# One chunk in 28 of two edge sums read row by row by the queues of ScalarE and SyncE

## What is computed

```python
def _gnn_layer(x, row, col, W, b, g, beta):
    neigh = x[col]
    agg = jax.ops.segment_sum(neigh, row, num_segments=n)
    deg = jax.ops.segment_sum(jnp.ones((row.shape[0],), x.dtype), row, num_segments=n)
    deg = jnp.maximum(deg, 1.0)[:, None]
    h = (x + agg / deg) @ W.T + b
    ...
x = _gnn_layer(x, row, col, W0, b0, g0, beta0)
x = _gnn_layer(x, row, col, W1, b1, g1, beta1)
```

## Time and profile before

| | us |
|---|---|
| median of three runs | 7440.92 |
| lowest and highest | 7439.2, 7442.39 |
| the profiled execution | 7400.07 |
| its span, first to last instruction | 7398.1 |
| granted TensorE clock, mean share of full | 0.714 |
| busy: PE, VectorE, POOL, ScalarE | 3606.4, 2823.8, 3772.0, 831.4 |

### The profile page before, as it was taken

The page is one execution under the profiler, slowest core; times in us unless marked ns, Lnnn a source line. Parts: engine busy times, 40 slices in busy tenths (PEclk is TensorE's granted clock), DMA queues, the critical chain, the costliest instruction groups (busy, mean ns, idle before and its releaser), DMA issues. The chain is left out here.

```text
span 7398.1 us, 63577 instructions
## 1 busy us (share of the span) xinstructions
PE 3606.4 (49%) x13693; PEld 2603.5 (35%) x13694; DVE 2823.8 (38%) x6837; ACT 831.4 (11%) x2066; POOL 3772.0 (51%) x3797
## 2 busy tenths in 40 slices
PE   4113965444433445445331222299992455555529
PEld 1001543333322333333230000078881344344317
DVE  5116854444435344444380000011114455555761
ACT  0001930000002000000130000022221100000222
POOL 4772046666662666666507777700005566667221
PEclk7556987777766777777655555599996777778759
DMA  3001023333311333332012000022214333333140
GB/s 134 1 0 37 13 58 92 93 92 91 92 42 47 92 91 93 92 93 84 5 38 91 2 4 4 9 72 81 81 57 135 90 91 92 90 90 92 55 160 18
DMA packets 290129, 497.38 MB, mean 67 GB/s; under 512 B 99253, under 2 KB 182880, under 8 KB 290048
## 3 DMA queue, kind: packets, MB, share of 16 engines
q0 software_dynamic: 163264, 345.19, 16.5%
q1 hardware_dynamic: 125696, 150.28, 6.3%
q10 hardware_dynamic: 1088, 1.05, 0.1%
HBM read 487.50 MB, written 92.89 MB: 78 GB/s over the span
## 5 line engine op out<-in xcount | busy, mean ns | idle before, releaser
L956 PE MATMUL sum_sums<-sum_got,sum_onehot 128*128 x4992 | 1627.4, 487 | 1717.5 <-DVE acc L1118 1317.3
L888 POOL DMA_INDIRECT sum_got<-xn,edge_row x1568 | 1539.5, 982 | 1139.8 <-issue 450.4
L956 PEld LDWEIGHTS sum_sums<-sum_got,sum_onehot 128*128 128x128 f32 x4992 | 1173.7, 245 | 2153.5 <-issue 1944.0
L1118 DVE TENSOR_TENSOR acc<-acc,sum_sums 128x257 f32 (+1 forms) x2496 | 1053.2, 422 | 1775.8 <-remote 1242.6
L888 POOL DMA_INDIRECT sum_got<-h,edge_row x784 | 753.9, 962 | 484.0 <-issue 226.3
L1256 POOL DMA_INDIRECT table<-rec,addr x784 | 807.8, 1030 | 291.5 <-issue 275.4
L1763 PE MATMUL moe_f_ps_y<-xb,moe_f_hT 128*128 128x256 f32 x1792 | 475.9, 398 | 297.7 <-issue 297.6
L1747 PE MATMUL moe_f_ps_h<-moe_f_xT,xb 128*128 128x256 f32 x1792 | 473.7, 398 | 286.5 <-issue 286.3
L1828 DVE TENSOR_TENSOR moe_f_y<-moe_f_ps_y,moe_b 128x256 f32<-128x256 f32 x112 | 42.3, 420 | 1337.2 <-PE moe_f_ps_y L1763 650.1
L1595 POOL DMA_INDIRECT moe_out_c_got<-moe_out,place_i x98 | 95.7, 976 | 826.2 <-PEq L1553 787.9
L1256 POOL DMA_INDIRECT table<-sort_rec,sort_addr x392 | 400.4, 1022 | 202.1 <-issue 122.5
(11 more groups left out here) (481 smaller groups left out, 3432.2 us busy)
## 6 DMA issues: line engine op xcount, KB each, us to landing
xb<-in_L_ffn_W SPq DMA_DIRECT2D x112, 1024.0 KB
sum_got<-xn,edge_row POOLq DMA_INDIRECT x1568
moe_in<-acc SPq DMA_DIRECT2D x28, 512.0 KB
moe_f_xin<-moe_in SPq DMA_DIRECT2D x56, 256.0 KB
moe_out<-moe_f_y SPq DMA_DIRECT2D x56, 256.0 KB
xn<-xb SPq DMA_DIRECT2D x14, 896.0 KB
table<-rec,addr POOLq DMA_INDIRECT x784
sum_got<-h,edge_row POOLq DMA_INDIRECT x784
```

What stands on the lines that cost most here:

```text
L888: pool.indirect_dma_start(got[:, c % SU, 0:D], None, source, bass.IndirectOffsetOnAxis(ap=p.edge_row[:, c:c + 1], axis=0)).then_inc(s_got[ ...
L956: mm = nc.tensor.matmul(sums[k % 2][j], onehot[:, (k % QUARTERS) * HALF + j, :], flat(got[:, bass.ds(where[n % PLAN], 1), :]), start=True, ...
L1118: v.tensor_tensor(a, a, sums[k % 2][j], ALU.add).then_inc(s_added[j], 1)
```

## The change

In sum0 and sum1, POOL leaves out the last chunk of each turn. Its 128 rows are fetched by 128 DMAs of one row each, whose row numbers are read into registers from a list: rows 0 to 71 by ACT's queue, in three batches of 24, rows 72 to 127 by SP's, in four batches of 14. The chunk has a slot of its own in odd turns (`got` has 29 slots), and the plan names the other slot for them, for which VectorE has three more operations. The row numbers stand in device memory in `row_list`, which SP writes once in sum0 (3584 numbers of 4 bytes, out of `edge_row`) and both engines read from, 72 or 56 numbers for each turn. ACT begins a turn's rows when `s_free` reaches four times the turn's number less 4, and in sum0 after its last clear. SP issues 14 rows behind each group's `s_landed`: behind the first two the second half of the turn under way, behind the last two the first half of the next. Before its first gate it issues the first half of turn 0. A turn counts as landed when both the 27 gathers and the 128 rows are in. Sum2 is not touched. Over both sums ACT issues 4032 such DMAs, SP 3136, and the lists take 112 small ones; POOL issues 56 gathers less.

```diff
@@ -44,6 +44,9 @@
 QW = CH
 BLOCK = 112
 BLOCKS = CH // BLOCK
+TURNS = CH // SU
+BY_ACT, ACT_BATCH = 72, 24
+BY_SP, SP_BATCH = 56, 14
 SE = 7
 FLYING = 7
 
@@ -727,7 +730,7 @@
     return eng.snap(register, min_val=1, max_val=most)
 
 
-def sum_over_edges(p, source, order, weighted, table, own=None):
+def sum_over_edges(p, source, order, weighted, table, own=None, by_row=None):
 
 
 
@@ -735,7 +738,10 @@
     with ExitStack() as ctx:
         cols = D if weighted else D + 1
         fields = 2 if weighted else 1
-        got = p.sb("got", [P, SU, cols], F32, ctx)
+
+
+        last_slot = SU - 1
+        got = p.sb("got", [P, SU + (by_row is not None), cols], F32, ctx)
         onehot = p.sb("onehot", [P, QUARTERS * HALF, P], F32, ctx)
         spare = p.sb("spare", [P, 4], F32, ctx)
 
@@ -752,6 +758,11 @@
         s_added = [s(f"s_added{j}") for j in range(HALF)]
         s_ready, s_built, s_onehot, s_sum = s("s_ready"), s("s_built"), s("s_onehot"), s("s_sum")
         s_landed, s_free = s("s_landed"), s("s_free")
+        if by_row is not None:
+            act_numbers, sp_numbers = p.sb("act_numbers", [1, 2, BY_ACT], I32, ctx), p.sb("sp_numbers", [1, 2, BY_SP], I32, ctx)
+            s_listed, s_room, s_known = s("s_listed"), s("s_room"), s("s_known")
+            s_act_list, s_sp_list, s_rows = ([s(f"{name}{odd}") for odd in range(2)]
+                                             for name in ("s_act_list", "s_sp_list", "s_rows"))
         if own is not None:
             own_rhs, own_biases = own
             own_row, own_flip = p.sb("own_row", [P, 2, D], F32, ctx), p.sb("own_flip", [P, 2, D], F32, ctx)
@@ -817,22 +828,71 @@
         def _(sp):
             if table is not None:
                 sp.dma_start(raw, table.rearrange("(p q) a -> p q a", p=P)).then_inc(s_raw, 16)
+            if by_row is not None and table is not None:
+                sp.wait_ge(s_table, 1)
+                sp.dma_start(by_row.rearrange("(c p) -> p c", p=P),
+                             p.edge_row[:].rearrange("p (c u) -> p c u", u=SU)[:, :, SU - 1],
+                             allow_slow_non_contiguous=True).then_inc(s_listed, 16)
+                sp.wait_ge(s_listed, 16)
+            if table is not None:
                 sp.wait_ge(s_plan, 3)
 
-            def step(i):
+            def read_list(turn, odd):
+                sp.dma_start(sp_numbers[:, odd, :], by_row[bass.ds(2 * P * turn + odd * P + BY_ACT, BY_SP)].unsqueeze(0)
+                             ).then_inc(s_sp_list[odd], 16)
+
+            def read_rows(turn, odd, quarter):
+                if quarter == 0:
+                    gate(sp, s_sp_list[odd], 16 * turn + 16, s_known)
+                first = quarter * SP_BATCH
+                _, row = nc.values_load_multi_w_load_instructions(
+                    sp_numbers[:, odd, first:first + SP_BATCH], (mybir.EngineType.SP,),
+                    min_val=0, max_val=NT * P - 1, skip_runtime_bounds_check_because="they are rows of the source")
+                for u in range(SP_BATCH):
+                    at = BY_ACT + first + u
+                    sp.dma_start(got[at:at + 1, last_slot + odd, 0:D],
+                                 source[bass.ds(row[u], 1), :]).then_inc(s_rows[odd], 16)
+
+            def step(i, rows_in=None):
                 _, used = nc.values_load_multi_w_load_instructions(
                     freed[:, bass.ds(GROUPS * i, GROUPS)], (mybir.EngineType.SP,), min_val=0, max_val=PIECES // HALF,
                     skip_runtime_bounds_check_because="the table counts groups of four pieces, from one up")
                 for h in range(GROUPS):
-                    if not (isinstance(i, int) and h < 2):
+                    if not (isinstance(i, int) and GROUPS * i + h < 2):
 
                         sp.wait_ge(s_sum, at_least_one(sp, used[h], PIECES // HALF))
                         sp.sem_inc(s_free, 1)
-                    gate(sp, s_got[h], 16 * EU * i + 16 * EU, s_landed)
-
-            step(0)
-            with sp.Fori(1, CH // SU) as i:
-                step(i)
+                    if h == GROUPS - 1 and by_row is not None:
+                        sp.wait_ge(s_got[h], 16 * (EU - 1) * i + 16 * (EU - 1))
+                        turn, odd, last = rows_in
+                        gate(sp, s_rows[odd], 16 * P * turn + 16 * P, s_landed)
+                    else:
+                        gate(sp, s_got[h], 16 * EU * i + 16 * EU, s_landed)
+                    if by_row is not None:
+                        turn, odd, last = rows_in
+                        if h < 2:
+                            read_rows(turn, odd, 2 + h)
+                            if h == 1 and not last:
+                                read_list(turn + 1, odd)
+                        elif not (last and odd):
+                            read_rows(turn + odd, 1 - odd, h - 2)
+
+            if by_row is not None:
+                for odd in range(2):
+                    read_list(0, odd)
+                for quarter in range(2):
+                    read_rows(0, 0, quarter)
+                for odd in range(2):
+                    step(odd, (0, odd, False))
+                with sp.Fori(1, TURNS // 2 - 1) as j:
+                    for odd in range(2):
+                        step(sp.snap(2 * j + odd), (j, odd, False))
+                for odd in range(2):
+                    step(TURNS - 2 + odd, (TURNS // 2 - 1, odd, True))
+            else:
+                step(0)
+                with sp.Fori(1, TURNS) as i:
+                    step(i)
 
         @block.scalar
         def _(act):
@@ -852,6 +912,39 @@
                 act.wait_ge(s_placed, 1)
                 clear(early, at)
 
+            def read_list(turn, odd):
+                act.dma_start(act_numbers[:, odd, :], by_row[bass.ds(2 * P * turn + odd * P, BY_ACT)].unsqueeze(0)
+                              ).then_inc(s_act_list[odd], 16)
+
+            def read_rows(turn, odd, last=False):
+                gate(act, s_act_list[odd], 16 * turn + 16, s_room)
+                for first in range(0, BY_ACT, ACT_BATCH):
+                    _, row = nc.values_load_multi_w_load_instructions(
+                        act_numbers[:, odd, first:first + ACT_BATCH], (mybir.EngineType.Activation,),
+                        min_val=0, max_val=NT * P - 1, skip_runtime_bounds_check_because="they are rows of the source")
+                    for u in range(ACT_BATCH):
+                        act.dma_start(got[first + u:first + u + 1, last_slot + odd, 0:D],
+                                      source[bass.ds(row[u], 1), :]).then_inc(s_rows[odd], 16)
+                if not last:
+                    read_list(turn + 1, odd)
+
+            def turns_by_row(turn, last=False):
+                for odd in range(2):
+                    gate(act, s_free, 2 * GROUPS * turn + (odd - 1) * GROUPS, s_room)
+                    read_rows(turn, odd, last)
+
+            if by_row is not None:
+                act.wait_ge(s_ready, 1)
+                if table is not None:
+                    act.wait_ge(s_listed, 16)
+                for odd in range(2):
+                    read_list(0, odd)
+                for odd in range(2):
+                    read_rows(0, odd)
+                with act.Fori(1, TURNS // 2 - 1) as j:
+                    turns_by_row(j)
+                turns_by_row(TURNS // 2 - 1, True)
+
             def step(i, owns):
                 for h in range(GROUPS):
                     q = h // 2
@@ -884,7 +977,7 @@
             for g in range(CH // EU):
                 if g >= GROUPS:
                     pool.wait_ge(s_free, g - GROUPS + 1)
-                for c in range(EU * g, EU * (g + 1)):
+                for c in range(EU * g, EU * (g + 1) - (by_row is not None and g % GROUPS == GROUPS - 1)):
                     pool.indirect_dma_start(got[:, c % SU, 0:D], None, source,
                                             bass.IndirectOffsetOnAxis(ap=p.edge_row[:, c:c + 1], axis=0)
                                             ).then_inc(s_got[g % GROUPS], 16)
@@ -942,8 +1035,8 @@
                     if k % QUARTERS == 0:
                         turn = flat(plan[:, bass.ds(2 * i + k // QUARTERS, 1), :])
                         _, where = nc.values_load_multi_w_load_instructions(
-                            turn[:, 0:PLAN], (mybir.EngineType.PE,), min_val=0, max_val=SU - 1,
-                            skip_runtime_bounds_check_because="the plan holds remainders by SU")
+                            turn[:, 0:PLAN], (mybir.EngineType.PE,), min_val=0, max_val=SU - (by_row is None),
+                            skip_runtime_bounds_check_because="the plan holds remainders by SU, and SU for the odd slot")
                         _, need = nc.values_load_multi_w_load_instructions(
                             turn[:, PLAN:], (mybir.EngineType.PE,), min_val=0, max_val=CH // EU,
```

(17 more changed lines are left out.)

## The result

The changed kernel takes 8295.65 us (median of six runs, 8292.0 to 8297.02) against 7440.06 for the kernel before, run beside it: a ratio of 1.115, interval 1.1135 to 1.1164. It is slower by 856 us. The forecast was 7492, in a range of 7390 to 7600.

What follows compares the result with a forecast made beforehand. POOL's gathers were taken to bound the kernel at 39.93 us a turn; with the change, ACT at 40.5. Later ends of sum0 (+35) and sum1 (+16) made +51 on 7440.92, so 7492 us, range 7390 to 7600.

Steps and rivals of the forecast that it cites:

- What bounds the kernel now: In sum0 and sum1 POOL sets the pace: 39.93 us a turn, 35.0 for 28 gathers and 4.9 for about two stops.
- what the change removes: One gather a turn on POOL in sum0 and sum1: 1.25 us less, 35 us a sum if the stops stay.
- What it adds on ScalarE: 72 one-row DMAs a turn on ACT at 0.475 us, plus 5.3 for loads and 1.0: 40.5 us a turn.
- rows 7, 8 and 10: Profile extracts: SP's one-partition DMAs (0.23, 0.25 us), SP's register-address DMAs (55 and 29 ns extra), ACT's weight loads (453 to 502 ns).
- On SP: SP's 14 rows and register load take 7.3 us a quarter, about 30 of 39.9 us a turn; they fit, costed at nothing.
- The one on SP: Rival: SP's row blocks hold back the frees POOL waits for, 42.3 us a turn, 7600 us; chance 0.08.
- A DMA that costs the queue far more: Rival: a one-row DMA takes 0.43 us, not 0.24, so ACT's turn is 51 us and the time 8080; chance 0.03.
- Code for ACT and SP: Rival: fetching loop code costs 1.1 us in each of 26 passes, +29, 7521 us; counted within the forecast's own range.
- rows 11: Profile extract on register loads, cited for code fetches: a 4-register load took up to 1.39 us for 0.30.
- Rows 9: Profile extract on SP's static DMAs, cited for code fetches and the dear DMA: up to 1.56 us where 0.43 was usual.
- Two ends of ACT's turn: Bounds on ACT's 40.5 us turn: 37.1 (0.43 a row) and 42.9 (0.49 a row and a code fetch each pass).
- the marks set for a failure: Wrong if ACT waits at s_free each turn, POOL's turn is under 39 us, or SP has no waits at 830.

## Why the prediction was wrong

**The direction was right by the wrong engine, and the size was out by a factor of 17.**

*What bounds the kernel now* and *what the change removes* held: 62 us for the two sums without rows, where 70 were worked out, with the stops unchanged.

*What it adds on ScalarE* is where the sum begins to fail. The row's price, 0.475 us, was put together from rows 7, 8 and 10, all of them from stretches in which POOL issues no gathers (the kernel's first microseconds, and 3700). For such a stretch it was even too high: 0.40 on ACT and 0.42 on SP with the gathers all but out, and 36.2 us a turn on ACT where the sum had 40.5. Beside the gathers it was 0.55 and 0.77. A price was carried from a quiet stretch into a busy one.

*On SP* is the step that failed outright. "The rows fit", at 7.3 us a block and 30 a turn, was 36.0 with the gathers all but out (four loads cost 8.7 us in place of 4.0, two of them being 3.06 us for their start; the rest 3.7) and 55.6 with them: 56 x 0.77 = 43.2 for the rows, 8.7 for loads, and 3.7 for the jump, the list and the gates. I costed at nothing what was the whole loss: 56 turns of 55.6 - 39.9 = 15.7 are 879 us, against 856 measured.

*The rivals.* The one on SP had the place and the direction (it named 0.55 us a row as the point from which it decides, and the row cost 0.77), but it was priced as one late free a turn and given 0.08. "A DMA that costs the queue far more" had an outcome near in size, 8080, by a cause that did not happen: the one-row DMA is 225 to 229 ns in the changed kernel too. The Trainium skill's 512 cycles (DMA: Bandwidth & Descriptors, the table of a later chip against earlier ones), 0.43 us by the prediction's estimate, are not what this chip's rows show. "Code for ACT and SP" was real, at 2.4 to 3.0 us a pass where 1.1 was taken, and too small to matter. Of its two signs, rows 11 were the gathers' doing and were read as code. Rows 9 are another matter: POOL has nothing to do from 740 to 765 us, so what made those DMAs take up to 1.56 us stays open. Two ends of ACT's turn were also added up slightly wrong, 37.1 for 37.3 and 42.9 for 42.1 us; nothing hangs on it.

The reading of rows 11 is the one to learn from. In the earlier trace rows a load of four registers takes 300 ns at the median and 1392 at most, within the sums. In the kernel before this cost nothing on SP, which had nothing else to do. It was the same slowness, seen on an engine with slack.

The range failed because each case in it took the idle price of an instruction; none let it change with what POOL was doing. Of the marks set for a failure two came true: SP's queue had no waits left at its old line 830 in the two sums, and ACT waited at `s_free` in nearly each turn. That "slower" came out is luck as far as ACT is concerned.

## What to carry to other kernels

Before an idle queue is given work beside another engine's gathers, look at what its few instructions cost there, at the maximum and not the median, and multiply by the number to be added. A queue's idle time is not spare if its instructions come slower in it. And a wait that breaks up the bursts of an engine that hinders the others can be worth more than it costs: here it gave back some 300 us.

## What the runs showed of the hardware

- While POOL issued indirect DMAs of 128 rows, 1.25 us apart, the instructions of SP's and ACT's queues, register moves and semaphore increments included, came with gaps of about 0.7 us, mostly one at a time, from some 3 us behind the first gather (0.7 with increments alone) to 1.0 to 2.4 us behind the last. The bytes gathered made no difference (8316 against 8296 us), memsets on POOL next to none (7227 against 7187). Long loops weren't needed for it: in the kernel before, SP's short loop shows the same gaps.
- In the kernel before, where VectorE and SP stood waiting for PE's count, it mostly came late: 6 us at the median behind the start of the matmul that raises it with POOL's bursts of 14 and 21 gathers; with one gather a group it was 0.68 us on VectorE.
- A DMA of one row of 1 KB at a register's address cost its queue 0.40 us on ACT and 0.42 on SP otherwise, with its two register instructions. ACT was not dearer than SP.
- A load of 14 registers took 3.06 us where it began 8 bytes off a multiple of 16, counted from the start of its list, and 1.2 to 1.3 where it began on one.
- Jumping back over a loop of 389 or 452 instructions took 2.4 to 3.0 us, over SP's loop of 45 instructions 0.17.

Left open: why POOL's gathers slow the others (what they share was not found), and by what way they hold back PE's count. That the count is behind the stops of the kernel before, 2.5 us and more, is read from its trace; no run changed it.
